# A four-stage sequence model in one kernel: pipeline streams shifted by a step, layer-norm means folded into the weights, and the state's weighing split in halves inside the recurrence's step

## The chip, the cores and the metric

The kernel runs on 1 core of a Trainium2 chip. The metric is device time in microseconds (us). Runs of one kernel agree here within 0.03%; the kernel before takes 3133.24 us (median of three, 3132.89 to 3133.72).

## The reference, cut to what matters

The input is 4 sequences of 1024 tokens with 128 features. Four blocks follow one another, each wrapped as x = layernorm(x + block(x)).

```python
# block 1: selective state space (256 inner channels, 16 states each)
h = exp(delta * A) * h + delta * b_t * u_t      # per channel and state, scanned over time
y = sum_over_states(h * c_t)                    # "the state's weighing"
# block 2: 16 routed experts (top 2) plus one shared expert, width 64 / 352
# block 3: an LSTM with 20 units over 1024 steps, then Gaussian attention
g = xg_t + h @ W_hh.T
c = sigmoid(f) * c + sigmoid(i) * tanh(gg);  h = sigmoid(o) * tanh(c)
# block 4: four MoE layers (4 experts of width 512, top 2)
logits = x @ rw + rb;  vals = top2(softmax(logits)) renormalised
xhat = (x - mean(x)) * rsqrt(mean((x - mean(x))**2) + 1e-5)
h = gelu((xhat * g + b) @ w1 + b1);  y = h @ w2 + b2;  x = sum_e comb_e * (x + y_e)
```

## The kernel before, in words

Time is cut into 8 chunks of 128 tokens (all 4 sequences at once, so a tile is 128 features x 512 columns, float32). The LSTM is the backbone: its 1024 steps cannot be made parallel, so everything else is placed between them. The function `period(i)` writes, for each engine, the instruction order of 128 steps of the LSTM (chunk i) and, between them, block 4 with the attention of chunk i-1 (`layer1`), block 2 of chunk i+1 (`layer0`), and the state-space scan of chunk i+2 (`scan`). Each stream is a Python generator that yields at the end of a slot; one slot holds one LSTM step. There is an opening (chunks 0 and 1 of blocks 1 and 2), periods 0 to 7, and a period 8 that has only `layer1`. Period 0 has no `layer1`, but it folds the layer-norm gain into w1 (`fold`). The scan runs in periods 0 to 5.

**A slot.** TensorE (PE) multiplies the last hidden state by w_hh (L905). ScalarE (ACT) takes the tanh of the gates (L915, L916). VectorE (DVE) does three small operations that end in the new cell (L929, L932, L935), ACT takes the cell's tanh (L919), and DVE writes the hidden state (L940), on which the next slot's PE waits. The tiles are p_turn (gates), cell, cell_t and hist.

**Block 4 in a period.** After 17 + q + 1 slots of attention come four layers of 23 slots. Five slots are the norm (mean by a matmul with mean_w, L623 and L625; centring on DVE, L372; square on ACT, L362; variance on PE; power -0.5 on GpSimd, L388; the product, L381). The routing decision lies beside it. Then come 18 slots of the experts: up matmul L656 into p_hid, Gelu L714, down matmul L666, and DVE's weighting L820 and sum L833.

**The scan in a period.** Sixteen slots of each layer (here called the heavy slots) carry 8 of the chunk's 32 scan steps. One scan step takes two slots, called a pair below. In the first slot DVE ends with the scan L1197 (state<-decay,drive). In the second it ends with the weighing L1206 (weighed<-state,rows). GpSimd (POOL) makes the next step's drive (L1135, then a small add L1139) and sums the weighed states into y (L1154). In the second slot of most pairs DVE also has one operation of block 4 (L820 or L833). The decays (ACT, L1226) are made in bursts in the norm's slots, and `layer0` advances in the slots that are not heavy.

Waits are semaphores. `put_drive` for step k+1 waits until scan k-1 is done, since two buffers take turns; `y` waits for the weighing.

Of the kernel before, what the change touches and what calls it, by code (L numbers as in the profile page):

```python
# [42 lines left out]
def body(nc, A, ctx, sem, out):  # L43
# [108 lines left out]
    w_router1 = sbuf("w_router1", [P, L * E1])  # L152
# [89 lines left out]
    fold_scaled = sem("r_fold_scaled")  # L242
    fold_stored = sem("r_fold_stored")
# [66 lines left out]
    g_step = sem("f1_step")  # L310
    g_comb = sem("f1_comb")
# [21 lines left out]
    def norm_pe(nm, n, src, ready, extra=None, early=None):  # L333
# [7 lines left out]
        if extra is not None:  # L341
            extra()
# [16 lines left out]
    def norm_act(nm, n):  # L359
        yield  # L360
        nc.scalar.wait_ge(nm.centred_done, n + 1)
# [6 lines left out]
    def norm_dve(nm, n, src, ready, dst):  # L368
        dve = nc.vector
        dve.wait_ge(*ready)  # L370
        dve.wait_ge(nm.mean_done, n + 1)
# [8 lines left out]
        dve.wait_ge(nm.centred_done, n + 1)  # L380
# [14 lines left out]
    def choose_dve(n, E, W, bank, bias, logit, left, top, mid, arg, half, mask, comb, tanh_, share_of, s_logit, s_step, s_arg, s_tanh, s_comb):  # L395
        dve = nc.vector
        dve.wait_ge(s_logit, n + 1)
        found = bank[:, 0:B * E].rearrange("p (b e) -> p b e", b=B)
# [15 lines left out]

# [6 lines left out]
        yield  # L421
# [14 lines left out]
    def layer0_pe(q):  # L436
# [24 lines left out]
        for u in range(U0):  # L461
# [32 lines left out]
    def layer0_act(q):  # L494
# [14 lines left out]
        yield  # L509
        for u in range(U0):  # L510
# [14 lines left out]
    def layer0_dve(q):  # L525
# [3 lines left out]
        yield from choose_dve(q, E0, E0, p_up, None, logit0, left0, top0, mid0, arg0, half0, mask0, comb0, tanh0, 0.25,  # L529
# [3 lines left out]
        nc.vector.tensor_scalar(share[:, :], share[:, :], 0.25, 0.25, ALU.mult, ALU.add).then_inc(share_ready, 1)  # L533
        yield
# [28 lines left out]
        weigh(U0 - 1)  # L563
        dve.wait_ge(down_done, (q + 1) * U0)
# [9 lines left out]
    LAYER = UN + 7  # L574
    att_slots = lambda q: 17 + q + 1
# [3 lines left out]
    def layer1_pe(q):  # L579
# [7 lines left out]
        for g in range(4):  # L587
            if g >= 2:
                pe.wait_ge(mup_taken, q * 4 + (g - 1))
            nc.tensor.matmul(p_hid[:, g % 2, :], w_mub[:, g, :], hist[:, q % 2, :, :], start=True, stop=True).then_inc(mup_done, 1)  # L590
            yield
# [4 lines left out]
        for i in range(q + 1):  # L596
# [3 lines left out]
            else:  # L600
                yield
# [12 lines left out]
        for _ in range(6):  # L614
            yield
# [3 lines left out]
        mm.then_inc(x3t_done, 1)  # L619
        yield  # L620
# [7 lines left out]
        for l in range(L):  # L628
# [42 lines left out]
    def layer1_act(q):  # L671
# [18 lines left out]
        for _ in range(9):  # L690
            yield
# [993 lines left out]
```

## Time and profile before

| | |
|---|---|
| median of three runs | 3133.24 us |
| profiled execution, its own time | 3143.73 us |
| its span | 3141.7 us |
| mean granted TensorE clock | 0.803 |
| busy: PE / DVE / ACT / POOL | 2537.0 / 1943.4 / 1386.7 / 1062.8 us |
| chain that ended last: PE / DVE / ACT / issue | 41% / 28% / 14% / 7% |

No engine is busy all the time: the LSTM's chain hands over between three of them in each slot. So what matters is read slot by slot: which engine's work ends last before the next hidden state. Starts of L905 mark the slots, and the stretches in the rows below begin and end at such starts. A "heavy" stretch is 16 slots and 8 scan steps long. A stretch between two heavy ones is 7 slots.

### The profile page before, as it was taken

What the parts mean: (1) busy time and instruction counts of PE and PEld (TensorE: products, weight loads), DVE (VectorE), ACT (ScalarE), POOL (GpSimd) and SP (SyncE); (2) the same over time, 40 slices, a digit from 0 to 9 for tenths busy, and PEclk for the clock granted to TensorE, in tenths of its full rate; (3) what the DMA queues carried; (4) which work ended last, traced back from release to release, by engine and by line L of the source; (5) the groups of instructions that cost most, each with busy time, mean ns of one, the idle gap of its engine ahead of it and who ended that gap; (6) DMA issues with size and microseconds to landing.
All of it is one profiled execution on the core that took longest, in us unless ns stands there. A gap on an engine that the chain in (4) does not pass through costs nothing.

```text
span 3141.7 us, 30770 instructions
## 1 busy us (share of the span) xinstructions
PE 2537.0 (81%) x7208; PEld 1271.2 (40%) x7208; DVE 1943.4 (62%) x6569; ACT 1386.7 (44%) x4620; POOL 1062.8 (34%) x913
## 2 busy tenths in 40 slices
PE   4776884479996989789886998788978997889598
PEld 1122443244444444344444443444444444444344
DVE  4857587357775777567766677577766555444422
ACT  3232433435544555445544554445534444444233
POOL 4735257104542445235432455244422001100200
PEclk7587655659996899878996899789978996788699
DMA  3231332003321233113220332122311220111021
GB/s 108 68 84 54 89 99 72 25 13 100 101 66 28 80 96 90 42 46 101 78 71 27 92 97 75 25 73 84 92 33 46 65 64 21 34 64 58 10 81 57
DMA packets 111774, 204.70 MB, mean 65 GB/s; under 512 B 14799, under 2 KB 24422, under 8 KB 111592
## 3 DMA queue, kind: packets, MB, share of 16 engines
q1 hardware_dynamic: 111592, 202.75, 22.1%
q8 instruction: 57, 0.93, 0.1%
q14 instruction: 125, 1.02, 0.1%
HBM read 195.36 MB, written 7.34 MB: 65 GB/s over the span
## 4 chain that ended last, share of the span: by engine, by line
PE 41%; DVE 28%; ACT 14%; issue 7%; POOL 1%; DVEq 0%; POOLq 0%; ACTq 0%
PE p_hid L656 8%; DVE state L1197 7%; PE p_turn L905 7%; PE p_misc L666 4%; ACT cell_t L919 4%; DVE cell L935 3%; DVE add_c L932 3%; PE p_acc L666 3%; DVE weighed L1206 2%; DVE p_turn L929 2%; PE p_misc L354 2%; PE p_gate L465 2%; DVE hist L940 2%; PE p_turn L475 1%; ACT cand L916 1%
## 5 line engine op out<-in xcount | busy, mean ns | idle before, releaser
L905 PEld LDWEIGHTS p_turn<-hist,w_hh 22*128 22x128 f32 x2048 | 371.6, 225 | 1148.2 <-DVE hist L940 1013.9
L905 PE MATMUL p_turn<-hist,w_hh 22*128 22x4 f32 x2048 | 457.3, 291 | 420.2 <-DVE hist L940 402.2
L656 PE MATMUL p_hid<-xhat,w 128*128 128x512 f32 x1024 | 581.8, 652 | 1.1 <-ACT hid L714 0.7
L919 ACT ACTIVATE cell_t<-cell 20x4 f32<-20x4 f32 x1024 | 207.7, 203 | 701.7 <-DVE cell L935 701.7
L1135 POOL TENSOR_TENSOR drive<-du,rows 128x512 f32<-128x512 f32 x256 | 473.4, 1849 | 63.2 <-DVE state L1197 44.9
L929 DVE SCALAR_TENSOR_TENSOR p_turn<-p_turn,cell 20x4 f32<-20x4 f32 x1024 | 170.7, 167 | 500.8 <-ACT p_turn L915 478.9
L714 ACT ACTIVATE hid<-p_hid,b1f 128x512 f32<-128x512 f32 x512 | 351.6, 687 | 243.1 <-PE p_misc L666 151.1
L388 POOL TENSOR_TENSOR n_rstd<-n_var,minus_half 128x4 f32<-128x4 f32 x56 | 62.0, 1108 | 1098.3 <-DVE n_var L376 1098.3
L1197 DVE TENSOR_TENSOR_SCAN state<-decay,drive 128x512 f32<-128x512 f32 x256 | 398.1, 1555 | 25.2 <-POOL drive L1139 15.7
L1154 POOL TENSOR_TENSOR y<-y,weighed 128x512 f32<-128x512 f32 x192 | 242.4, 1262 | 450.5 <-DVE weighed L1206 449.9
L940 DVE SCALAR_TENSOR_TENSOR hist<-p_turn,cell_t 20x4 f32<-20x4 f32 x1024 | 162.7, 159 | 275.6 <-ACT cell_t L919 275.6
L915 ACT ACTIVATE p_turn<-p_turn 96x4 f32<-96x4 f32 x1024 | 157.8, 154 | 349.1 <-PE p_turn L905 345.7
L666 PE MATMUL p_acc<-hid,w 128*128 128x512 f32 x512 | 275.3, 621 | 0.0
L666 PE MATMUL p_misc<-hid,w 128*128 128x512 f32 x512 | 264.1, 598 | 0.0
L1206 DVE TENSOR_TENSOR weighed<-state,rows 128x512 f32<-128x512 f32 x256 | 184.7, 722 | 7.9 <-DVE state L1197 0.5
L916 ACT ACTIVATE cand<-p_turn 32x4 f32<-32x4 f32 x1024 | 171.9, 168 | 25.2
L935 DVE SCALAR_TENSOR_TENSOR cell<-p_turn,add_c 20x4 f32<-20x4 f32 x1024 | 157.9, 154 | 35.3
L656 PEld LDWEIGHTS p_hid<-xhat,w 128*128 128x128 f32 x1024 | 160.3, 191 | 42.5 <-issue 26.5
L1169 PE MATMUL p_hid<-weighed,ident 128*128 128x512 f32 x128 | 113.7, 986 | 78.9 <-DVE weighed L1206 78.9
L1226 ACT ACTIVATE decay<-delta,a_neg 128x508 f32<-128x508 f32 x256 | 174.6, 710 | 2.2
L932 DVE SCALAR_TENSOR_TENSOR add_c<-p_turn,cand 20x4 f32<-20x4 f32 x1024 | 154.8, 151 | 31.6
L1139 POOL TENSOR_TENSOR drive<-drive,kc 128x4 f32<-128x4 f32 x256 | 143.2, 559 | 20.1
(204 smaller groups left out, 3161.5 us busy)
## 6 DMA issues: line engine op xcount, KB each, us to landing
rows<-rows_dram SPq DMA_DIRECT2D x128, 512.0 KB, 5.0
w<-w_dram SPq DMA_DIRECT2D x128, 256.0 KB, 2.7
w<-in_w2T SPq DMA_DIRECT2D x128, 256.0 KB, 2.7
comb_b<-comb_dram SPq DMA_DIRECT2D x64, 512.0 KB, 4.7
rows<-comb_dram SPq DMA_DIRECT2D x128, 128.0 KB, 2.9
w<-in_w1T SPq DMA_DIRECT2D x16, 256.0 KB, 2.8
w_dram<-w SPq DMA_DIRECT2D x16, 256.0 KB, 2.4
out_xT<-result SPq DMA_DIRECT2D x8, 256.0 KB, 2.5
```

What stands on the lines that cost most here:

```text
L656: nc.tensor.matmul(p_hid[:, v % 2, :], w1[:, v // FB, (v % FB) * P:(v % FB + 1) * P], xhat[:, :], start=True, stop=True).then_inc(g_h, 1)
L666: nc.tensor.matmul((p_misc1, p_acc1)[e % 2][:, :], w2[:, e, f, :], hid1[:, w % 2, :], start=(f == 0), stop=(f == FB - 1)).then_inc(g_y, 1)
L714: nc.scalar.activation(hid1[:, v % 2, :], p_hid[:, v % 2, :], ACT.Gelu, bias=b1f[:, l * UN + v:l * UN + v + 1]).then_inc(g_gelu, 1)
L905: nc.tensor.matmul(gate_bank(i)[:, :, t:t + 1], w_hh[:, :], before, start=False, stop=False, skip_group_check=True).then_inc(gates_done, 1)
L919: nc.scalar.activation(cell_t[64:64 + PE_, :], cell[32:32 + PE_, :], ACT.Tanh, scale=0.5).then_inc(cell_tanh, 1)
L929: nc.vector.scalar_tensor_tensor(out=gate(32), in0=gate(32), scalar=1.0, in1=cell[32:32 + PE_, :], op0=ALU.add, op1=ALU.mult).then_inc(kee ...
L932: nc.vector.scalar_tensor_tensor(out=add_c[32:32 + PE_, :], in0=gate(0), scalar=1.0, in1=cand[0:PE_, :], op0=ALU.add, op1=ALU.mult).then_i ...
L935: nc.vector.scalar_tensor_tensor(out=cell[32:32 + PE_, :], in0=gate(32), scalar=0.5, in1=add_c[32:32 + PE_, :], op0=ALU.mult, op1=ALU.add) ...
L1135: nc.gpsimd.tensor_tensor(flat(drive[:, n % 2, :, :]), du[:, j, :], rows[:, (u * S + s_) % ROWS, 0, :], ALU.mult).then_inc(driven, 1)
L1154: nc.gpsimd.tensor_tensor(y[:, j, :], y[:, j, :], weighed[:, n % 2, :], ALU.add).then_inc(y_summed, 1)
L1197: nc.vector.tensor_tensor_scan(flat(state[:, n % 2, :, :]), flat(decay[:, n % RING, :, :]), flat(drive[:, n % 2, :, :]), 0.0, ALU.mult, AL ...
L1206: nc.vector.tensor_tensor(weighed[:, n % 2, :], flat(state[:, n % 2, :, :]), rows[:, (u * S + s_) % ROWS, 1, :], ALU.mult).then_inc(weighe ...
```

## The change

- **Weighing.** The 512 columns of L1206 are split in two halves of 256. In periods they are written by a new stream, `mamba_gap_dve`, that stands between the LSTM's cell and its output: half one in the slot after the scan, half two one slot later, ahead of the next scan. Only half two signals `weighed_done`. In the opening the weighing stays whole.
- **The sum into y.** GpSimd (or PE in the opening) now sums step k-1 after it has made the drive of step k+1; before, it summed step k.
- **Centred weights.** The fold in period 0 subtracts the column mean from w1 (one matmul and one subtraction more for each of 16 tiles), so block 4's norm needs no centring: a fifth column in the router's matmul gives the mean, the square is taken of x itself, and the variance is E[x^2] + eps - mean^2. The two matmuls with mean_w and the centring go from the four layers; the last norm keeps them.
- **Order.** The transposes of the routing weights and their copy move behind the first up matmul; two DVE operations of the attention become one; decays stand ahead of the layer's work in their slots; `layer0` starts at slot 1 (was 4) and skips the last slot of each layer; several streams have a yield more or less.

```diff
     def choose_dve(...):
...
                                        in1=logit[:, :, 0:E], op0=ALU.mult, op1=ALU.add).then_inc(s_arg, 1)
-
+        yield
         nc.vector.memset(top[:, :, 2:8], -NEVER).then_inc(s_step, 1)
...
     def layer1_pe(q):
...
-            ln = norm_pe(n1, q * NL + l, src, (n1.src_ready, q * NL + l + 1), logits, (lambda: mean_of_two(n)) if l else None)
-            for s_ in range(5):
-                next(ln)
-                if s_ == 4:
-                    pe.wait_ge(g_comb, n + 1)
...
+            pe.wait_ge(n1.src_ready, q * NL + l + 1)
+            for j in range(B):
+                mm = nc.tensor.matmul(p_hid[:, 0, j * (E1 + 1):(j + 1) * (E1 + 1)], tile(src, j), w_router1[:, l, :],
+                                      start=True, stop=True)
+            mm.then_inc(g_logit, 1)
+            yield
+            pe.wait_ge(n1.square_done, q * NL + l + 1)
...
     def layer1_act(q):
...
+            nc.scalar.activation(n1.square[:, :], src, ACT.Square).then_inc(n1.square_done, 1)
...
     def layer1_dve(q):
...
+            nc.vector.scalar_tensor_tensor(out=n1.var[:, :], in0=p_acc1[:, 448:448 + B], scalar=EPS, in1=mean1[:, :],
+                                           op0=ALU.add, op1=ALU.subtract).then_inc(n1.var_taken, 1)
...
+            nc.vector.tensor_tensor(xhat[:, :], src, p_misc1[:, :], ALU.mult).then_inc(n1.out_done, 1)
...
     def lstm_dve(i):
...
             nc.vector.scalar_tensor_tensor(out=cell[32:32 + PE_, :], in0=gate(32), scalar=0.5,
                                            in1=add_c[32:32 + PE_, :], op0=ALU.mult, op1=ALU.add).then_inc(cell_done, 1)
+            yield
             dve.wait_ge(cell_tanh, n + 1)
...
     def mamba_scan_pool(u, early):
         pool = nc.gpsimd
+
+        def sum_y(k):
+            n, j = u * NS + k, k % NB
+            pool.wait_ge(weighed_done, n + 1)
+            if k < NB:
+                pool.wait_ge(y_begun, u * NB + j + 1)
+            else:
+                pool.wait_ge(y_summed, n - 1)
+            nc.gpsimd.tensor_tensor(y[:, j, :], y[:, j, :], weighed[:, n % 2, :], ALU.add).then_inc(y_summed, 1)
+
         for k in range(NS):
             n, j = u * NS + k, k % NB
             if k + 1 < NS:
                 put_drive(u, k + 1)
             yield
-            if not early:
...
+            if not early and k:
+                sum_y(k - 1)
+            yield
+        if not early:
+            sum_y(NS - 1)
...
+    def weigh_state(u, k, at, to):
...
+        cols = slice(at * CH, to * CH)
+        mm = nc.vector.tensor_tensor(weighed[:, n % 2, cols], flat(state[:, n % 2, :, :])[:, cols],
+                                     rows[:, (u * S + s_) % ROWS, 1, cols], ALU.mult)
+        if to == B:
+            mm.then_inc(weighed_done, 1)
+
+    def mamba_gap_dve(u):
+        for k in range(NS):
+            yield
+            weigh_state(u, k, 0, B // 2)
+            yield
+            weigh_state(u, k, B // 2, B)
...
     def fold_pe():
...
+            pe.wait_ge(fold_grown, k + 1)
+            if k:
+                pe.wait_ge(fold_scaled, k)
+            nc.tensor.matmul(p_misc1[:, :], mean_w[:, :], w1[:, k % E1, :], start=True, stop=True).then_inc(fold_mean, 1)
...
     def fold_dve():
...
+            dve.wait_ge(fold_mean, k + 1)
+            nc.vector.tensor_tensor(w1[:, k % E1, :], w1[:, k % E1, :], p_misc1[:, :], ALU.subtract).then_inc(fold_scaled, 1)
...
-    L0_AT = 4
+    L0_AT = 1
+    BURST = {LAYER - 1: 1, 0: 1, 1: 2, 2: 2, 3: 2}
...
             next(lstm, None)
+            o = (slot - att) % LAYER
+            heavy = layer1 is not None and slot >= att and NORM + 1 <= o < LAYER - 1 and slot < tail
+            if u < NCH:
+                if layer1 is None and soft[1] > SOFT and done["gap"] <= SCAN:
+                    advance(gap, "gap", SCAN)
+                elif layer1 and (heavy or slot == tail):
+                    advance(gap, "gap", SCAN)
+            next(lstm, None)
...
-            if layer0 and not (heavy and slot < CH) and slot >= (L0_AT if layer1 else 0):
+            last = layer1 is not None and att < slot < tail and o == LAYER - 1
+            if layer0 and not ((heavy or last) and slot < CH) and slot >= (L0_AT if layer1 else 0):
                 next(layer0, None)
```

**DVE in one pair of heavy slots.** Before: keep, add, cell, output (hist), then the layer's sum and the weighing; the second slot ends in the scan.

```order
L929 SCALAR_TENSOR_TENSOR p_turn<-p_turn,cell 20x4
L932 SCALAR_TENSOR_TENSOR add_c<-p_turn,cand 20x4
L935 SCALAR_TENSOR_TENSOR cell<-p_turn,add_c 20x4
L940 SCALAR_TENSOR_TENSOR hist<-p_turn,cell_t 20x4
L833 TENSOR_TENSOR part<-part,terms 128x512
L1206 TENSOR_TENSOR weighed<-state,rows 128x512
L929 SCALAR_TENSOR_TENSOR p_turn<-p_turn,cell 20x4
L932 SCALAR_TENSOR_TENSOR add_c<-p_turn,cand 20x4
L935 SCALAR_TENSOR_TENSOR cell<-p_turn,add_c 20x4
L940 SCALAR_TENSOR_TENSOR hist<-p_turn,cell_t 20x4
L1197 SCALAR_TENSOR_TENSOR state<-decay,drive 128x512
```

The same pair after the change (the line numbers are those of the changed kernel: L1282 is the weighing, L1264 the scan, L876 the sum).

```order
L978 SCALAR_TENSOR_TENSOR p_turn<-p_turn,cell 20x4
L981 SCALAR_TENSOR_TENSOR add_c<-p_turn,cand 20x4
L984 SCALAR_TENSOR_TENSOR cell<-p_turn,add_c 20x4
L1282 TENSOR_TENSOR weighed<-state,rows 128x256
L990 SCALAR_TENSOR_TENSOR hist<-p_turn,cell_t 20x4
L876 TENSOR_TENSOR part<-part,terms 128x512
L978 SCALAR_TENSOR_TENSOR p_turn<-p_turn,cell 20x4
L981 SCALAR_TENSOR_TENSOR add_c<-p_turn,cand 20x4
L984 SCALAR_TENSOR_TENSOR cell<-p_turn,add_c 20x4
L1282 TENSOR_TENSOR weighed<-state,rows 128x256
L990 SCALAR_TENSOR_TENSOR hist<-p_turn,cell_t 20x4
L1264 SCALAR_TENSOR_TENSOR state<-decay,drive 128x512
```

The weighing has left its place behind the sum; its two halves stand ahead of the output in both slots, and the second half is two instructions ahead of the next scan.

**POOL in the heavy slots**, after the change; the rows read as before it, with L1135, L1139 and L1154 for L1188, L1192 and L1204.

```order
L1188 TENSOR_TENSOR drive<-du,rows 128x512 [waits m_scan_done,m_rows_loaded0]
L1192 TENSOR_TENSOR drive<-drive,kc 128x4 [waits m_kc_done,m_driven]
L1204 TENSOR_TENSOR y<-y,weighed 128x512 [waits m_y_summed,m_weighed_done]
L1188 TENSOR_TENSOR drive<-du,rows 128x512 [waits m_scan_done,m_rows_loaded1]
L1192 TENSOR_TENSOR drive<-drive,kc 128x4 [waits m_kc_done,m_driven]
```

What moved is the step that the sum belongs to: behind the drive of step k+1 it is now step k-1's, whose weighing ends just ahead of scan k.

**PE at the start of a layer's norm**, before:

```order
L623 MATMUL p_misc<-part,mean_w 128x512
L625 MATMUL p_misc<-terms,mean_w 128x512
L634 MATMUL p_hid<-w_router,xl 128x4 x4
L475 MATMUL p_turn<-hid0w,w_down 128x512
L905 MATMUL p_turn<-hist,w_hh 128x4
```

and after:

```order
L645 MATMUL p_hid<-w_router,xl 128x5 x4
L470 MATMUL p_up<-mid_x,w_up 128x512
L952 MATMUL p_turn<-hist,w_hh 128x4
L651 MATMUL p_acc<-mean_w,esig 128x1 x4
L476 MATMUL p_turn<-hid0w,w_down 128x512
```

The two 512-column matmuls with mean_w are gone from the slot; `layer0`'s matmuls stand in it as before.

## Rows read from the trace of the kernel before

**Rows 1.** The page: granted TensorE clock by 40 slices of the span, in tenths.

```profile
PEclk7587655659996899878996899789978996788699
```

**Rows 2.** The scan's line: count, duration ns (min/median/max), first and last start.

```profile
L1197 DVE TENSOR_TENSOR_SCAN state<-decay,drive x256: 1210/1392/2289, 53.3 to 2300.0; 128x512 f32<-128x512 f32 x128
```

**Rows 3.** Windows of period 3: length, busy by engine (PE, PEld, DVE, ACT, POOL), clock.

```profile
1392.98:1431.38 38.40, 34.73 (x92) 14.75 (x93) 30.42 (x86) 19.73 (x72) 26.57 (x21) 1.00 0.36 112
1431.38:1457.32 25.94, 24.13 (x65) 12.39 (x65) 15.10 (x63) 13.25 (x36) 3.72 (x4) 0.68 0.14 44
1457.32:1495.62 38.30, 34.73 (x94) 14.75 (x93) 29.79 (x85) 19.37 (x72) 26.57 (x21) 1.00 0.44 122
1495.62:1515.97 20.35, 18.11 (x65) 9.18 (x65) 14.48 (x63) 12.78 (x36) 4.22 (x4) 0.92 0.11 41
1515.97:1554.71 38.74, 34.73 (x92) 14.75 (x92) 30.43 (x86) 20.21 (x74) 26.58 (x21) 1.00 0.39 122
...
1575.41:1612.29 36.88, 34.74 (x93) 14.76 (x93) 30.22 (x87) 18.33 (x72) 24.34 (x19) 1.00 0.33 97
```

**Rows 4.** Windows: period 0 with fold and layer0; its 11 last scans; period 6, heavy.

```profile
364.34:476.96 112.62, 97.26 (x239) 54.45 (x239) 91.73 (x220) 40.53 (x154) 54.36 (x47) 0.55 0.32 96
...
495.95:541.50 45.55, 12.87 (x45) 10.94 (x45) 35.65 (x111) 17.28 (x83) 42.32 (x33) 0.50 0.12 37
...
2413.15:2447.99 34.84, 34.03 (x92) 14.75 (x93) 14.42 (x71) 17.70 (x64) 0.00 (x0) 1.00 0.26 79
```

**Rows 5.** Timeline of one pair of heavy slots: start us, duration us, engine.

```profile
1534.51 0.16 DVE L940 SCALAR_TENSOR_TENSOR hist<-p_turn,cell_t 20x4 f32<-20x4 f32 x1 [0.27 <-ACT cell_t L919]
...
1534.70 0.69 DVE L833 TENSOR_TENSOR part<-xl,terms 128x512 f32<-128x512 f32 x1
...
1535.28 0.16 ACT L915 ACTIVATE p_turn<-p_turn 96x4 f32<-96x4 f32 x1
1535.31 0.69 DVE L1206 TENSOR_TENSOR weighed<-state,rows 128x512 f32<-128x512 f32 x1
...
1536.07 1.26 POOL L1154 TENSOR_TENSOR y<-y,weighed 128x512 f32<-128x512 f32 x1 [0.62 <-DVE weighed L1206]
...
1536.83 0.16 DVE L940 SCALAR_TENSOR_TENSOR hist<-p_turn,cell_t 20x4 f32<-20x4 f32 x1 [0.27 <-ACT cell_t L919]
1537.02 1.39 DVE L1197 TENSOR_TENSOR_SCAN state<-decay,drive 128x512 f32<-128x512 f32 x1
...
1537.29 2.18 POOL L1135 TENSOR_TENSOR drive<-du,rows 128x512 f32<-128x512 f32 x1
...
1538.44 0.17 DVE L929 SCALAR_TENSOR_TENSOR p_turn<-p_turn,cell 20x4 f32<-20x4 f32 x1
...
1538.83 0.15 DVE L935 SCALAR_TENSOR_TENSOR cell<-p_turn,add_c 20x4 f32<-20x4 f32 x1
...
1539.25 0.16 DVE L940 SCALAR_TENSOR_TENSOR hist<-p_turn,cell_t 20x4 f32<-20x4 f32 x1 [0.27 <-ACT cell_t L919]
```

**Rows 6.** Timeline: a scan that starts just behind a GpSimd operation.

```profile
1403.20 1.26 POOL L1135 TENSOR_TENSOR drive<-du,rows 128x512 f32<-128x512 f32 x1
1403.34 2.20 DVE L1197 TENSOR_TENSOR_SCAN state<-decay,drive 128x512 f32<-128x512 f32 x1
```

**Rows 7.** Timeline of the opening: a weighing behind a drive.

```profile
202.26 1.56 POOL L1135 TENSOR_TENSOR drive<-du,rows 128x512 f32<-128x512 f32 x1 [4.10 <-DVE state L1197]
202.61 1.75 DVE L1206 TENSOR_TENSOR weighed<-state,rows 128x512 f32<-128x512 f32 x1
```

**Rows 8.** Timeline where a layer's norm begins.

```profile
1436.12 1.97 PE L623 MATMUL p_misc<-part,mean_w 128*128 128x512 f32 x2
...
1437.92 1.02 PE L625 MATMUL p_misc<-terms,mean_w 128*128 128x512 f32 x2
...
1439.05 0.69 DVE L372 TENSOR_TENSOR mdrive<-xl,p_misc 128x512 f32<-128x512 f32 x1 [1.68 <-PE p_misc L625]
```

More of the change, by code:

```diff
@@ L517, in layer0_act @@
                 yield
+        for _ in range(3):
+            yield
+        yield from norm_act(n0, 2 * q + 1)
         yield
-        yield from norm_act(n0, 2 * q + 1)
         act.wait_ge(xt_done, q + 1)
@@ L586, in layer1_pe @@
         pe.wait_ge(xm_done, min(q + 3, NCH))
[L587 to L590, printed above, removed]
+        for k, g in enumerate((0, 2, 1, 3)):
+            if k >= 2:
+                pe.wait_ge(mup_taken, q * 4 + (k - 1))
+            nc.tensor.matmul(p_hid[:, k % 2, :], w_mub[:, g, :], hist[:, q % 2, :, :], start=True, stop=True).then_inc(mup_done, 1)
             yield
@@ L613, in layer1_pe @@
         mm.then_inc(ss_summed, 1)
-        for _ in range(6):
+        for _ in range(7):
             yield
@@ L657, in layer1_pe @@
                                      start=True, stop=True).then_inc(g_h, 1)
+                if v == 0:
+                    pe.wait_ge(g_comb, n + 1)
+                    for j in range(B):
+                        mm = nc.tensor.transpose(tile(p_acc1, j)[0:E1, :], comb1[:, j, :], ident[:, :])
+                    mm.then_inc(g_combT, 1)
                 if v >= 2:
@@ L689, in layer1_act @@
             yield
-        for _ in range(9):
+        for _ in range(10):
             yield
@@ L803, in layer1_dve @@
         mm.then_inc(nt_done, 1)
-        yield
-        yield
+        for _ in range(3):
+            yield
         for l in range(L):
@@ L892, in layer0_pool @@
         yield from norm_pool(n0, 2 * q)
-        for _ in range(6 + 3 * U0):
+        for _ in range(9 + 3 * U0):
             yield
@@ L990, in mamba_pre_pe @@
         yield
+        z(1, p_misc1)
         yield
@@ L1425, in period @@
         ends = att + L * LAYER + 5 if layer1 else 0
-        done = dict(scan=0, leave=0, fold=0, pre=0, soft=0)
+        done = dict(scan=0, leave=0, fold=0, pre=0, soft=0, gap=0)
         fold_slots = 3 * L * E1 + 12 + 1
@@ L1439, in period @@
             next(lstm, None)
+            o = (slot - att) % LAYER
[6 more added lines that the diff above has]
+            next(lstm, None)
+            if u < NCH and layer1 and att - 1 <= slot < tail - 2:
+                for _ in range(BURST.get(o, 0)):
+                    next(burst, None)
             if layer1:
                 next(layer1, None)
-            o = (slot - att) % LAYER
-            heavy = layer1 is not None and slot >= att and 6 <= o < LAYER - 1 and slot < tail
-            if layer0 and not (heavy and slot < CH) and slot >= (L0_AT if layer1 else 0):
+            last = layer1 is not None and att < slot < tail and o == LAYER - 1
+            if layer0 and not ((heavy or last) and slot < CH) and slot >= (L0_AT if layer1 else 0):
                 next(layer0, None)
@@ L1606, in start @@
                 dve.sem_inc(h_ready, 1)
-            of = dict(soft=mamba_soft_dve, scan=mamba_scan_dve, leave=mamba_leave_dve, fold=fold_dve, layer0=layer0_dve,
+            of = dict(soft=mamba_soft_dve, scan=mamba_scan_dve, gap=mamba_gap_dve, leave=mamba_leave_dve, fold=fold_dve, layer0=layer0_dve,
                       layer1=layer1_dve, lstm=lstm_dve)
```

247 lines of the change are left out of this document (142 added, 105 removed).

## The prediction, made before the changed kernel was run

> **What bounds the kernel now.** I read three views in this order. The slices of the page show the clock going up and down, so the run is a row of stages with different limits [rows 1]. Windows cut at the starts of L905 then give the length of each stage. The timeline of two slots, last, shows what ends last in one.
>
> A heavy stretch has 16 slots and 8 scan steps. The four of period 3 take 38.40, 38.30, 38.74 and 36.88 us, 152.3 us together [rows 3], or 4.76 us for a pair of slots. In period 6, which has no scan, the same 16 slots take 34.84 us with PE busy for 34.03 [rows 4]. So PE's floor is 4.36 us a pair, and the scan costs 0.40 us on top. Five periods have such stretches, 20 in all, with 160 pairs: of the 256 scans [rows 2], 64 lie in the opening and 32 in period 0.
>
> Within a pair DVE ends last in both slots [rows 5]. In the scan's slot the hidden state is out at 1536.99, the scan runs from 1537.02 to 1538.41, keep starts 0.03 us later, the cell ends 0.54 us after that, and the next hidden state is out at 1539.41: 2.42 us. In the other slot the sum (0.69) and the weighing (0.69) stand in a row ahead of keep, and the slot takes 2.32 us. ACT's gates end at 1535.44, before DVE is free.
>
> **The rows that decide: DVE and GpSimd hold each other up.** The scan of [rows 5] takes 1.39 us, with the last 0.31 us of GpSimd's y beside its start; with nothing on GpSimd it is 1.21 us at the least [rows 2]. The drive that GpSimd starts 0.27 us into it takes 2.18 us instead of 1.26 and ends 1.06 us after the scan: it has waited. In [rows 6] the order is reversed. The drive starts 0.14 us ahead of the scan and takes its plain 1.26, and the scan takes 2.20. In [rows 7] a weighing starts 0.35 us behind a drive and takes 1.75 us, ending 0.54 us after the drive. The LSTM's small operations, which read PSUM, run beside a drive at their usual 0.15 to 0.17 us [rows 5]. So an operation of DVE with two SBUF tensors that starts behind a GpSimd operation waits for its end.
>
> The Trainium skill (SBUF — State Buffer, "SBUF: two separate sides") states this as an exclusive lock that the first one holds for its whole instruction. By that rule too the next paragraph's order of starts is what matters; the trace agrees with it in both directions [rows 5 to 7].
>
> **The weighing in halves.** Half of L1206 is 256 columns. No row has that shape. Between the 0.16 us of a four-column operation and the 0.69 of 512 columns it is 0.42 us [rows 5]; the bounds are half of 0.69, 0.35, and all of it. The gap between cell and output is 0.27 us [rows 5], so an undisturbed half delays the output by 0.03 + 0.42 + 0.03 - 0.27 = 0.2 us.
>
> The Trainium skill (VectorE: DVE Perf Modes, "The TRN2 errata") gives 58 cycles plus one per column at 0.96 GHz for such an operation, 0.33 us for a half; its sum would be about 15 us lower. For 512 columns that is 0.59, and the rows show 0.69, so I keep to the rows.
>
> Now the order of starts in a pair after the change, counted from the output in the slot of scan k, time 0:
> - Half two of step k-1 ends 0.19 us before 0 (0.03 of hand-over and 0.16 for the output). It releases y(k-1) on GpSimd, which has long ended its drive. A weighing's end is followed by y's start in 0.07 us [rows 5], so y starts at -0.12 and the scan, at +0.03, is 0.15 us behind. That is the distance of [rows 6]. The scan takes 2.20 us, to 2.23.
> - The drive of step k+2 waits for this scan. It starts about 0.1 us later and runs its 1.26 us, to 3.59. Keep to cell take 0.03 + 0.54 us, so half one of step k asks at 2.83, behind the drive. It ends 0.27 us after the drive (0.54 of [rows 7] less half the columns), at 3.86. The output follows, to 4.05.
> - In the next slot the layer's operation (0.03 + 0.75 at most) covers the gates, which end 0.77 us after an output [rows 5]; keep starts at 0.81, the cell ends at 1.35, half two at 1.80, the output at 1.99. GpSimd is idle by then.
>
> The pair takes 4.05 + 1.99 = 6.04 us, of 8 in a stretch six with a layer operation and two 0.1 shorter: 48.1 against 38.1. What was removed, a 0.69 us weighing ahead of keep, is in this sum. Twenty stretches cost 20 x 10.1 = **+202 us**. Queued behind the held scan and half are the LSTM's own operations, so nothing hides it. The bounds are -52 us, if nothing collides (the first rival), and +240, if a half took 0.6.
>
> **Clock.** PE then works some 4.4 of 6.04 us, with an idle stretch of about 1.9 in each pair. The stretch 1431.38 to 1457.32 has PE busy 24.13 of 25.94 us at a granted 0.68, the heavy ones stand at 1.00 [rows 3]. At 1.2 GHz a pair of passes takes 1.97 us against 1.02 [rows 8], and a pair of slots would take about 8 us. If 15% of 20 x 48 us ran at that level it would cost 960 x 0.15 x (1 - 6.04/8) = **+35 us**. The bounds are 0 and 85 (35%).
>
> **Period 0.** No layer operation stands there, and the eleven last scans take 45.55 us, 4.14 us a pair [rows 4]. At 6.0 us they cost +20, four pairs ahead of them +5. In the first 112.62 us [rows 4] `layer0` operations stand between output and scan, so y has mostly run out by then. There the fold adds 16 subtractions of 0.69 us and 16 matmuls; PE, 86% busy at 0.55 of the clock, has little room. I take +8 (0 to 25). Sum **+33 us**.
>
> **The norm.** The mean's two matmuls take PE from 1436.12 to 1438.78, DVE sits idle 1.68 us for them, and the centring takes 0.69 [rows 8]. At full clock they are about 1.8 us, and they stand in the slot that begins a norm. The slot before it also loses `layer0`'s matmul, about 1.2 us. I count -3 us for each of 20 norms, -60; `layer0` comes back in the attention's first slots for +2 a period, +10. Period 6 and 7 give -14 (1.8 a norm, no more), period 8, where the norm is a bare chain, 4 x -1.8 = -8. Sum **-72 us** (bounds -110 and -40). What is late next is PE's logits and `layer0` matmul in the same slot. The mean's copy, its square and the fifth column are 0.2 us of DVE beside other work; the Square of x instead of the centred tile costs the same. The moved transposes lie behind an up matmul; the copy of the weights for the DMA is a slot later, and is first used five slots on: 0. The decays moved within their slots: 0, or +1 us a norm if they hold up the square.
>
> **The rest.** One 0.69 us operation of DVE fewer in each attention: 8 x -0.69 = **-5 us**. The later sum into y in the opening changes no wait, as step k-2 is still summed a step ahead of its buffer's next use: 0. The shifted yields of the pre and leave streams keep the number of slots: 0, give or take 5.
>
> **Sum.** 202 + 35 + 33 - 72 - 5 = +193 us on the profiled execution's 3143.73, 3337. That execution is 10.5 us above the median of 3133.24, so in the median's terms 3326.
>
> **Rivals.**
> 1. *No collision*: y or the scan gets in first without holding up the other, or the lock does not work at this distance. Then the scan's slot is 0.03 + 1.21 + 0.57 + 0.45 + 0.19 = 2.45 and the other 1.99, 4.44 a pair. PE's floor is 4.36, so a stretch is 35.5: -52 us. With +10 for period 0, no clock term and -77 for norm and attention: -119, **3014 us**. This is the other side. For it speaks that the weighing leaves DVE's longest slot; against it [rows 6], at nearly the same distance. It decides from 5.2 us a pair down: there 160 pairs cost 0.45 x 160 = 70 us, what the norm saves.
> 2. *Only the scan is held up* (the drive comes later than half one): 3.44 + 1.99 = 5.43 a pair, 43.4 a stretch, +106; with +15 of clock, +20 and -77: **3197 us**. [rows 7] speak against it, since half one asks 0.6 us after the scan and the drive needs only a semaphore.
> 3. *Only half one is held up*: 3.06 + 1.99 = 5.05, 40.2 a stretch, +42; with +5, +20 and -77: -10, **3123 us**. It needs GpSimd still busy when half two ends, and nothing in the order gives it work there.
>
> **Chances.** The forecast 0.78, rival 1 0.13, rival 2 0.05, rival 3 0.02, anything slower still 0.02. The forecast's own range is 3200 to 3430: the heavy stretches +180 to +220, the clock 0 to +85, the norm -110 to -40. Rival 2 lies at its edge, so the range starts at 3190; rivals 1 and 3 stay outside. About 0.2% can be told from no change here: faster 0.15, same 0.01, slower 0.84.
>
> **What would show it.** The scan's group in the periods at a mean near 2.2 us instead of 1.4; the weighing's halves in two kinds, 0.42 and about 1.0 us; y starting 0.1 to 0.2 us ahead of a scan; heavy stretches near 48 us with slots of 4.1 and 2.0 in turn; no L623 in layers 1 to 3, and stretches between heavy ones some 3 us shorter. Scans of 1.2 to 1.4 us and stretches of 36 us would make the prediction wrong by its first step; a clock of 1.00 in the heavy stretches would take away the clock's term alone.

## The result, and the profile after

The changed kernel takes 3416.7 us (median of four runs, 3414.01 to 3420.31) where the kernel before takes 3133.48 (3132.89 to 3136.19): a ratio of 1.0903, with a 95% interval of 1.0884 to 1.0922. It is slower by 283 us; 193 were forecast. The profiled execution is 3414.01 us, its span 3412.2, 270.5 above the span before. The first four runs of the kernel before agree within 0.11%; in the experiments below it takes 3127.14 to 3156.39 us, with medians of 3141.53 to 3146.63, so differences of a few tenths of a per cent between experiments mean little.

The page first: busy time by engine, the granted clock in 40 slices, and four groups (busy us, mean ns, idle time ahead and what ended most of it).

```profile
PE 2681.1 (79%) x7128; PEld 1336.5 (39%) x7128; DVE 2212.1 (65%) x6802; ACT 1398.1 (41%) x4620; POOL 906.0 (27%) x914
...
PEclk6686665578886888868886878968876898587788
...
L1264 DVE TENSOR_TENSOR_SCAN state<-decay,drive 128x512 f32<-128x512 f32 x256 | 522.5, 2041 | 23.8 <-POOL drive L1192 14.4
...
L1188 POOL TENSOR_TENSOR drive<-du,rows 128x512 f32<-128x512 f32 x256 | 348.3, 1360 | 311.5 <-DVE state L1264 294.6
...
L1204 POOL TENSOR_TENSOR y<-y,weighed 128x512 f32<-128x512 f32 x192 | 242.5, 1263 | 530.2 <-DVE weighed L1282 530.2
L1282 DVE TENSOR_TENSOR weighed<-state,rows 128x256 f32<-128x256 f32 (+1 forms) x448 | 325.4, 726 | 18.8 <-DVE state L1264 0.5
```

The scan's mean over all 256 is 2041 ns for 1555 before, its median 2200 for 1392 [rows 2]. Both means hold 64 scans of the opening at about 1.9 us; in the heavy stretches alone the mean is 2.17 us for 1.43, and 155 of the 160 scans there take over 2 us, for 14 before. GpSimd is busy for 157 us less than before: its drive no longer waits behind a running scan, it makes DVE wait. Its idle time ahead of y (530 us) is all put down to the weighing, that ahead of the drive (295 of 312) to the scan: each starts as soon as DVE signals. DVE's 269 us more of "busy" (2212.1 for 1943.4) are mostly time in which it is held up: 124 us in the scans and some 110 in the halves, whose split by itself costs about 0.15 us a step.

The timeline of a pair shows the order of starts.

```profile
1539.89 0.42 DVE L1282 TENSOR_TENSOR weighed<-state,rows 128x256 f32<-128x256 f32 x1
...
1540.35 0.16 DVE L990 SCALAR_TENSOR_TENSOR hist<-p_turn,cell_t 20x4 f32<-20x4 f32 x1
1540.39 1.26 POOL L1204 TENSOR_TENSOR y<-y,weighed 128x512 f32<-128x512 f32 x1 [2.00 <-DVE weighed L1282]
...
1540.66 2.08 DVE L1264 TENSOR_TENSOR_SCAN state<-decay,drive 128x512 f32<-128x512 f32 x1 [0.15 <-issue]
...
1542.88 1.26 POOL L1188 TENSOR_TENSOR drive<-du,rows 128x512 f32<-128x512 f32 x1 [1.23 <-DVE state L1264]
...
1543.34 1.08 DVE L1282 TENSOR_TENSOR weighed<-state,rows 128x256 f32<-128x256 f32 x1
1544.43 0.16 DVE L990 SCALAR_TENSOR_TENSOR hist<-p_turn,cell_t 20x4 f32<-20x4 f32 x1
...
1545.92 0.42 DVE L1282 TENSOR_TENSOR weighed<-state,rows 128x256 f32<-128x256 f32 x1
1546.37 0.16 DVE L990 SCALAR_TENSOR_TENSOR hist<-p_turn,cell_t 20x4 f32<-20x4 f32 x1
1546.42 1.26 POOL L1204 TENSOR_TENSOR y<-y,weighed 128x512 f32<-128x512 f32 x1 [1.94 <-DVE weighed L1282]
...
1546.56 2.20 DVE L1264 TENSOR_TENSOR_SCAN state<-decay,drive 128x512 f32<-128x512 f32 x1
```

Read it by starts. Half two ends at 1540.31; y starts 0.08 us later, the scan 0.27 us after y, and the scan ends 1.09 us after y. The drive starts 0.14 us after the scan's end; half one, 0.46 us behind the drive, takes 1.08 us and ends 0.28 after it. Half two, with an idle GpSimd, takes 0.42. The outputs end at 1540.51, 1544.59 and 1546.53: slots of 4.08 and 1.94 us. The scan at 1540.66 is one of two that start so late; the other 153 held scans start 0.14 to 0.2 us behind y, as the one at 1546.56 does, and take 2.20 us.

The windows of period 3 answer to [rows 3]: length, busy by engine, clock.

```profile
1502.52:1521.97 19.45, 18.48 (x55) 10.05 (x55) 11.22 (x56) 12.54 (x33) 2.45 (x3) 0.65 0.13 42
1521.97:1568.43 46.46, 36.03 (x94) 15.33 (x93) 40.90 (x93) 19.29 (x72) 19.51 (x21) 0.96 0.31 94
1568.43:1592.37 23.94, 22.43 (x59) 12.11 (x59) 13.37 (x62) 13.71 (x36) 2.46 (x3) 0.57 0.13 44
1592.37:1640.03 47.66, 36.03 (x94) 15.32 (x93) 42.51 (x94) 19.38 (x73) 20.77 (x22) 0.96 0.35 100
1640.03:1663.99 23.96, 22.37 (x58) 12.13 (x58) 13.37 (x62) 13.71 (x36) 2.46 (x3) 0.57 0.07 22
```

And two of period 0 answer to [rows 4]:

```profile
361.34:483.05 121.71, 96.28 (x252) 48.92 (x251) 110.56 (x247) 40.87 (x153) 46.12 (x50) 0.68 0.30 89
509.50:575.90 66.40, 12.84 (x45) 10.90 (x45) 53.36 (x121) 17.30 (x83) 27.57 (x29) 0.50 0.09 24
```

A heavy stretch went from about 38.1 to about 47.2 us, and its clock fell only to 0.96. The seven slots between two heavy stretches got longer together (71.87 us for 66.99 in period 3), although they hold less work: they stand at a clock of 0.57, which before was 0.68 to 0.92. The next table adds such windows up over each kernel's profiled execution (us; e1 to e7 are experiments, below).

| part | before | after | e1 | e2 | e5 | e6 | e7 |
|---|---|---|---|---|---|---|---|
| opening | 327.9 | 318.8 | 317.4 | 322.2 | 319.4 | 320.2 | 323.5 |
| period 0 | 318.4 | 361.8 | 331.1 | 352.0 | 328.8 | 330.5 | 329.3 |
| periods 1-5, heavy | 761.9 | 946.9 | 748.3 | 958.6 | 748.3 | 745.0 | 747.8 |
| periods 1-5, between (norm and last slots) | 443.1 | 459.4 | 444.3 | 432.7 | 420.4 | 435.6 | 416.3 |
| periods 1-5, attention and tail | 484.5 | 508.6 | 502.8 | 485.3 | 497.9 | 498.3 | 497.0 |
| period 6 | 303.5 | 315.4 | 319.6 | 307.7 | 309.5 | 305.5 | 311.0 |
| period 7 | 293.7 | 291.8 | 294.8 | 297.1 | 285.0 | 292.0 | 282.8 |
| period 8 | 208.7 | 209.4 | 209.5 | 209.5 | 210.3 | 209.5 | 210.4 |

### The profile page after: what moved, and what is told of

It reads as the page before. It is cut to its first block, busy times and chain, and to the rows that moved or that the text cites. A ratio compares the mean times of both kernels' runs of the same rounds, so it can differ in the third digit from the quotient of the medians.

```text
span 3412.2 us, 30859 instructions
## 1 busy us (share of the span) xinstructions
PE 2681.1 (79%) x7128; PEld 1336.5 (39%) x7128; DVE 2212.1 (65%) x6802; ACT 1398.1 (41%) x4620; POOL 906.0 (27%) x914
## 4 chain that ended last, share of the span: by engine, by line
PE 42%; DVE 33%; issue 8%; ACT 8%; POOL 1%; DVEq 0%; POOLq 0%; ACTq 0%
DVE state L1264 11%; PE p_hid L668 8%; PE p_turn L952 7%; DVE weighed L1282 5%; PE p_misc L685 3%; DVE add_c L981 3%; PE p_acc L685 3%; PE p_up L470 3%; PE p_gate L466 2%; DVE cell L984 2%; PE p_turn L476 2%; DVE hist L990 2%; PE p_misc L657 2%; ACT cell_t L968 2%; DVE p_turn L978 2%
## 5 line engine op out<-in xcount | busy, mean ns | idle before, releaser
L952 PEld LDWEIGHTS p_turn<-hist,w_hh 22*128 22x128 f32 x2048 | 388.9, 235 | 1309.8 <-DVE hist L990 1030.4
L952 PE MATMUL p_turn<-hist,w_hh 22*128 22x4 f32 x2048 | 475.2, 300 | 503.6 <-DVE hist L990 503.3
L668 PE MATMUL p_hid<-xhat,w 128*128 128x512 f32 x1024 | 602.3, 672 | 4.9 <-DVE xhat L857 4.9
L1264 DVE TENSOR_TENSOR_SCAN state<-decay,drive 128x512 f32<-128x512 f32 x256 | 522.5, 2041 | 23.8 <-POOL drive L1192 14.4
L1188 POOL TENSOR_TENSOR drive<-du,rows 128x512 f32<-128x512 f32 x256 | 348.3, 1360 | 311.5 <-DVE state L1264 294.6
L1204 POOL TENSOR_TENSOR y<-y,weighed 128x512 f32<-128x512 f32 x192 | 242.5, 1263 | 530.2 <-DVE weighed L1282 530.2
L1282 DVE TENSOR_TENSOR weighed<-state,rows 128x256 f32<-128x256 f32 (+1 forms) x448 | 325.4, 726 | 18.8 <-DVE state L1264 0.5
L685 PE MATMUL p_acc<-hid,w 128*128 128x512 f32 x512 | 283.8, 639 | 0.0
L932 POOL TENSOR_TENSOR n_rstd<-n_var,minus_half 128x4 f32<-128x4 f32 x32 | 32.4, 1011 | 800.8 <-DVE n_var L850 800.8
L466 PE MATMUL p_gate<-mid_x,w_gate 128*128 128x512 f32 x176 | 147.4, 933 | 15.5 <-DVE hid L564 13.2
```

What stands on the lines that cost most here:

```text
L668: nc.tensor.matmul(p_hid[:, v % 2, :], w1[:, v // FB, (v % FB) * P:(v % FB + 1) * P], xhat[:, :], start=True, stop=True).then_inc(g_h, 1)
L685: nc.tensor.matmul((p_misc1, p_acc1)[e % 2][:, :], w2[:, e, f, :], hid1[:, w % 2, :], start=(f == 0), stop=(f == FB - 1)).then_inc(g_y, 1)
L952: nc.tensor.matmul(gate_bank(i)[:, :, t:t + 1], w_hh[:, :], before, start=False, stop=False, skip_group_check=True).then_inc(gates_done, 1)
L1188: nc.gpsimd.tensor_tensor(flat(drive[:, n % 2, :, :]), du[:, j, :], rows[:, (u * S + s_) % ROWS, 0, :], ALU.mult).then_inc(driven, 1)
L1204: nc.gpsimd.tensor_tensor(y[:, j, :], y[:, j, :], weighed[:, n % 2, :], ALU.add).then_inc(y_summed, 1)
L1264: nc.vector.tensor_tensor_scan(flat(state[:, n % 2, :, :]), flat(decay[:, n % RING, :, :]), flat(drive[:, n % 2, :, :]), 0.0, ALU.mult, AL ...
```

## The experiments

Theory A, as the expectations call it, is the prediction's: GpSimd's y starts just ahead of the scan and holds it, and the drive then holds half one. Theory B is that the halves are harmless and the new norm and order cost the time. Each experiment gives the ratio to the kernel before in the same batch, with its 95% interval.

**e1: the weighing whole and in its old place**, the rest of the change kept.

```diff
-            if not early and k:
-                sum_y(k - 1)
+            if not early:
+                sum_y(k)
...
-            if early:
-                weigh_state(u, k, 0, B)
+            weigh_state(u, k, 0, B)
...
-            weigh_state(u, k, 0, B // 2)
...
-            weigh_state(u, k, B // 2, B)
```

> The changed kernel with the weighing whole and at its old place (behind the layer's operation) and GpSimd summing step k again, all else of the change kept. Theory A (DVE and GpSimd hold each other up: y ahead of the scan, the drive ahead of half one): scans fall from 2.20 back to about 1.4 us, the heavy stretches from 189 us a period to 152, period 0 loses some 35 us, so 3417 - 185 - 35 = about 3197 us. If the slow norms of the changed kernel come from the idle PE of its heavy stretches, they get faster too and it is 3150. Theory B (the halves are harmless, the new norm and order cost the time): within 20 us of 3417.

Measured: 3169.61 us against 3146.63, ratio 1.0069 (1.0044 to 1.0094). The heavy stretches fall from 946.9 to 748.3 us. So the weighing's new place explains nearly the whole loss; but what is left of the change, which the prediction priced at a gain of some 70 us, loses 0.7%. The time lies between the two that were expected, 3150 and 3197 us.

**e2: the weighing's part alone**, on the kernel before.

```diff
+            if not early and k:
+                sum_y(k - 1)
...
+    def mamba_gap_dve(u):
+        for k in range(NS):
+            yield
+            weigh_state(u, k, 0, B // 2)
+            yield
+            weigh_state(u, k, B // 2, B)
```

> The kernel before with only the halves between cell and output and GpSimd's sum one step later; norm, fold and order of before. Theory A: 160 pairs in periods 1 to 5 from 4.76 to 5.9 us, +185, and period 0 +30: about 3350 us, with scans at 2.20 us. Theory B: about 3135 to 3170 us (the halves' overflow of 0.2 us a slot at most). A third reading, in which half of the loss is the norm's, would also give 3350 here, but then e1_whole stays near 3197.

Measured: 3356.25 us, ratio 1.0668 (1.0637 to 1.0699), heavy stretches 191.7 us a period, mean of all scans 2057 ns. Most of the loss comes with this part alone. The whole change loses 9.0%, more than 6.7% and e1's 0.7% together. In the profiled executions the excess is 21 us (270 for 223 and 26), and the norm and last slots account for it: +16 us, for -10 in e2 and +1 in e1.

**e3: y held back until the scan is done**, so that nothing runs on GpSimd when the scan starts.

```diff
         def sum_y(k):
             n, j = u * NS + k, k % NB
+            if k + 1 < NS:
+                pool.wait_ge(scan_done, n + 2)
             pool.wait_ge(weighed_done, n + 1)
```

> The changed kernel, but GpSimd's sum of step k-1 also waits until scan k is done, so it cannot start ahead of that scan. Theory A, with two separate collisions: scans fall to 1.2 us, half one stays held up at about 1.1 us (now by y), a pair goes from 5.9 to about 5.05 us, 160 x -0.85 = -136, period 0 -12: about 3270 us. Theory B: no change, or a few us more for the later sum.

Measured: 3262.11 us, ratio 1.0363 (1.0334 to 1.0393). Its timeline:

```profile
1478.96 1.23 DVE L1266 TENSOR_TENSOR_SCAN state<-decay,drive 128x512 f32<-128x512 f32 x1
...
1480.32 1.26 POOL L1206 TENSOR_TENSOR y<-y,weighed 128x512 f32<-128x512 f32 x1 [2.16 <-DVE state L1266]
1480.80 1.06 DVE L1284 TENSOR_TENSOR weighed<-state,rows 128x256 f32<-128x256 f32 x1
```

The scan runs free in 1.23 us. Half one is now behind y, and ends 0.28 us after it. One collision of the two is gone, and with it 5.4% of the time (1.0903 to 1.0363). Not all of this is the collision's own: of the 153 us between the two profiled executions, 107 lie in the heavy stretches and 13 in period 0, but 31 in the norm and last slots, where the granted clock is 0.70 for 0.61.

**e8 and e9: the weighing whole, between cell and output of the next scan's slot.** Nothing then stands in the gap of the slot that the drive fills. In e9 y is free to start; e8 has e3's wait as well.

```diff
     def mamba_gap_dve(u):
...
             yield
-            weigh_state(u, k, 0, B // 2)
             yield
-            weigh_state(u, k, B // 2, B)
+            weigh_state(u, k, 0, B)
```

> The changed kernel with the weighing whole between cell and output, in the slot of the next scan alone (nothing in the other slot), and GpSimd's sum of step k-1 held until scan k is done. Collision theory: the scan runs free (1.2 us), GpSimd then does y and the drive in a row (2.6 us), and the weighing, asking some 3.5 us after the scan's start, meets only the tail of the drive: a pair of 4.6 to 4.9 us, heavy stretches of 147 to 156 us a period, total as e1_whole or a few us from it (3150 to 3185 us). If placing the weighing in the gap were itself what costs, it would stay near e3's 3262 us.

> The changed kernel with the weighing whole between cell and output in the slot of the next scan, none in the other slot, and GpSimd's sum free to start (no added wait). Collision theory: only the scan is held up (y starts 0.14 us ahead of it, scans at 2.20 us); the drive's end no longer meets a weighing. From the measured slots: the scan's slot 3.2 to 3.3 us, the other 2.3 (0.27 us of gap, 0.69 of weighing), a pair of 5.5 us, heavy stretches of 176 us a period, 13 us a period less than the changed kernel's 189: about 3345 us, ratio 1.065 to 1.072. If the two collisions did not add up one by one, it would stay at 1.09 or fall to 1.03.

Measured: e8 3168.85 us, ratio 1.0095 (1.0062 to 1.0127); e9 3312.7, ratio 1.0548 (1.0512 to 1.0584). The timeline of e9:

```profile
1492.39 0.69 DVE L1282 TENSOR_TENSOR weighed<-state,rows 128x512 f32<-128x512 f32 x1
1493.11 0.16 DVE L990 SCALAR_TENSOR_TENSOR hist<-p_turn,cell_t 20x4 f32<-20x4 f32 x1
1493.16 1.26 POOL L1204 TENSOR_TENSOR y<-y,weighed 128x512 f32<-128x512 f32 x1 [1.31 <-DVE weighed L1282]
1493.30 2.20 DVE L1264 TENSOR_TENSOR_SCAN state<-decay,drive 128x512 f32<-128x512 f32 x1
```

The weighing is free, y starts 0.14 us ahead of the scan, the scan is held. The heavy stretches came as expected (175 us a period for 176), the total 32 us below the expected 3345: period 0 is 16 us shorter than in the changed kernel, norm and last slots 9, attention and tails 7, and the expectation had counted none of these. With e3, e8 and the changed kernel this makes a square (the scan's time is the mean in the heavy stretches):

| heavy stretches, us a period | y waits for the scan | y free |
|---|---|---|
| whole weighing in the gap | e8: 151.5, scan 1.23 us | e9: 175, scan 2.17 us |
| halves in the gap | e3: 168, scan 1.23 us | after: 189, scan 2.17 us |

The held scan alone costs 23 us a period, the held half alone 16, both 38. Work in the gap by itself costs next to nothing: e8, whose weighing is still held, for about 0.4 us in 43 of the 160 pairs, stands beside e1's 149.7. So neither the split nor the gap costs much by itself; what costs is which engine starts first.

**e4 and e5: the two matmuls with mean_w put back, their result unread**, in layers 1 to 3; e4 on the changed kernel, e5 on e1.

```diff
+            if l:
+                pe.wait_ge(g_summed, n * E1 - 1)
+                nc.tensor.matmul(p_misc1[:, :], mean_w[:, :], part[:, :], start=True, stop=False, skip_group_check=True)
+                pe.wait_ge(g_weighted, n * E1)
+                nc.tensor.matmul(p_misc1[:, :], mean_w[:, :], terms[:, (E1 - 1) % 2, :], start=False, stop=True,
+                                 skip_group_check=True)
```

> The changed kernel with the two matmuls with mean_w put back at the start of the norm of layers 1 to 3, as work that nothing reads (the result stays the same). Clock theory (the emptier PE around the start of the norm lets the granted clock fall, and the whole norm then runs at the lower level): the stretches between heavy ones get a clock of 0.7 to 0.9 instead of 0.57 and stay at 24 us or fall to 22, so 3400 to 3420 us. Work theory (each matmul costs what it takes, no more): 24 norms x 1.8 to 3.7 us = 3460 to 3500 us.

> e1_whole (weighing whole, at its old place, all else of the change) with the two unread matmuls with mean_w at the start of the norm of layers 1 to 3. Clock theory: as e4 did against the changed kernel, the unread work gives time back: the stretches between heavy ones at a clock near 0.75 instead of 0.6, ratio to the kernel before 0.995 to 1.002 (e1_whole: 1.007). Work theory: 24 x 1.8 us or more on top, ratio 1.02.

Measured: e4 3398.6 us, ratio 1.0774 (1.0723 to 1.0824), below the changed kernel's 1.0903; e5 3129.74 us against 3141.53, ratio 0.9966 (0.9945 to 0.9988), below e1's 1.0069. By these ratios, adding work that nobody reads made both kernels 1% faster. In us it is 40 for e5 against e1 (1.3%), but only 18 for e4 against the changed kernel (0.5%), because the kernel before was 13 us slower beside e4; that pair is the weaker evidence. Windows of e1, the seven slots between heavy stretches, three times in period 3:

```profile
1440.88:1462.40 21.52, 18.54 (x58) 10.09 (x58) 13.70 (x63) 13.65 (x36) 4.38 (x6) 0.76 0.13 41
1499.80:1523.08 23.28, 21.02 (x59) 11.74 (x59) 13.97 (x63) 13.91 (x36) 4.38 (x6) 0.63 0.07 23
1560.47:1582.00 21.53, 18.48 (x58) 10.10 (x58) 13.61 (x63) 13.65 (x36) 4.38 (x6) 0.76 0.09 25
```

The same three in e5:

```profile
1427.08:1449.85 22.77, 21.64 (x62) 11.18 (x62) 14.07 (x63) 13.91 (x36) 4.38 (x6) 0.70 0.15 44
1487.27:1507.15 19.88, 17.15 (x62) 9.09 (x63) 13.97 (x63) 13.81 (x36) 4.38 (x6) 0.91 0.08 27
1544.56:1563.55 18.99, 17.08 (x62) 8.62 (x63) 13.61 (x63) 13.65 (x36) 4.39 (x6) 0.91 0.10 29
```

Summed, e1 takes 66.33 us with 175 matmuls and 58.03 us of busy PE, e5 61.64 us with 186 matmuls and 55.87 us busy. More matmuls in less busy time: the clock was granted at 0.91 in two of three stretches, in e1 in none. DVE's and ACT's busy times differ by under 0.5 us.

**e6 and e7: `layer0` allowed in the last slot of a layer again**; e6 on e1, e7 on e5.

```diff
-            if layer0 and not ((heavy or last) and slot < CH) and slot >= (L0_AT if layer1 else 0):
+            if layer0 and not (heavy and slot < CH) and slot >= (L0_AT if layer1 else 0):
```

> e1_whole with the block-2 stream (layer0) allowed again in the last slot of each layer, so that one 512-column matmul stands in the slot just ahead of the norm, as in the kernel before. Clock theory: the clock at the start of the norm stays up more often, the first two slots of the norm (5.2 and 4.2 us) shrink by 1 to 2 us in most of 24 norms, ratio 0.995 to 1.003. If only the work counts: the slot grows by about 1 us and an attention or tail slot shrinks by as much, ratio 1.005 to 1.009.

> e5 and e6 together: weighing whole, the unread mean matmuls, and layer0 in the last slot. If both work by the clock and add up: ratio 0.985 to 0.995. If one of them already fills the gap: as the better of the two. Work theory: the slowest of the three, 1.02.

Measured: e6 3135.06 us, ratio 0.9974 (0.9954 to 0.9994); e7 3108.11 us, ratio 0.9899 (0.987 to 0.9928). The unread matmuls give time back, `layer0`'s old place gives time back, and both together most. But e6 adds no work for PE, it only moves it (7128 matmuls, as e1 has), and its gain is not all the clock's: in the norm and last slots it is 9 us shorter than e1 at the same clock of 0.69, in period 6 it is 14 us shorter at 0.85 for 0.79. e7 beats the kernel before by 1.0% and is the best of all. Its three stretches of period 3:

```profile
1431.65:1452.16 20.51, 19.36 (x65) 10.19 (x65) 14.53 (x64) 13.72 (x36) 4.38 (x6) 0.83 0.19 52
1489.57:1509.65 20.08, 18.00 (x64) 9.72 (x64) 14.56 (x64) 14.21 (x37) 4.51 (x6) 0.92 0.09 27
1546.15:1567.60 21.45, 18.08 (x60) 9.91 (x61) 13.88 (x63) 13.22 (x35) 4.38 (x6) 0.77 0.08 26
```

## Why the prediction was right about the heavy stretches, and short by 90 us

**Heavy stretches: forecast +202, and +35 for the clock; measured +185.** The order of starts came as written: y, then the scan at 2.20, then the drive, then half one. The forecast slots were 4.05 and 1.99 us, the two in the timeline 4.08 and 1.94. Over all 160 pairs the mean is 5.92. The scan's slot takes 4.09 us in most pairs; but the last scan of a stretch has no drive behind it, its half one runs free in 0.42, and its slot takes 3.43. The other slot, behind the first of a stretch, takes 1.84 to 2.20, by what block 4 has in it. When half one asks later (0.72 us instead of 1.08, at 1549.73) the slot is as long, since the half still ends 0.28 us after the drive. A half took 0.42 us when free, as interpolated from the rows. The 0.33 comes from a general row of the cited section; the same section of the Trainium skill (VectorE: DVE Perf Modes, "The TRN2 errata") says that this row comes out too low and gives (columns + 151) cycles at 0.96 GHz for an fp32 tensor_tensor add, which for 256 columns makes 0.42. Rival 1 fell with the 155 scans of over 2 us. Rivals 2 and 3 exist as experiments: only the scan held, 5.46 us a pair in e9 (forecast 5.43, there with the halves split); only the half held, 5.25 in e3 (forecast 5.05, with half one behind a drive that starts on time; in e3 it stands behind y).

**Period 0: forecast +33, measured +43.** The eleven last scans take 66.40 us for 45.55 [rows 4], 6.04 a pair, for a forecast of 6.0. The stretch of [rows 4] with the fold took +9.1, against +8 forecast. The eight slots between the two windows took +7.5 (26.45 us for 18.99), against +5, and the 36 us ahead of both took +6, for which I had counted nothing. e1 puts the change without the weighing at +12.7 in this period.

**The norm: forecast -72, of it -60 for periods 1 to 5; measured +16 in their norm and last slots. This is the step that failed.** I took PE's matmuls off at what they cost and left the clock of what remained as it was. e1 puts +1 of the 16 to the change without the weighing, where -60 was forecast; beside it the weighing's new place adds the other 15. Part of what took the gain is the clock. The table has the three stretches of period 3, and in its last two columns all norm and last slots of periods 1 to 5, with the mean granted clock in them:

| kernel | matmuls | length, us | PE busy, us | clock | all norm and last slots, us | clock there |
|---|---|---|---|---|---|---|
| before | 194 | 66.99 | 61.80 | 0.68, 0.92, 0.84 | 443.1 | 0.81 |
| after | 176 | 71.87 | 67.13 | 0.57, 0.57, 0.57 | 459.4 | 0.61 |
| e2 | 193 | 63.99 | 58.68 | 0.78, 0.92, 0.83 | 432.7 | 0.83 |
| e3 | 175 | 67.36 | 61.83 | 0.62, 0.76, 0.57 | 428.2 | 0.70 |
| e4 | 188 | 68.50 | 63.33 | 0.60, 0.77, 0.83 | 450.4 | 0.70 |
| e1 | 175 | 66.33 | 58.03 | 0.76, 0.63, 0.76 | 444.3 | 0.69 |
| e6 | 177 | 66.09 | 59.09 | 0.76, 0.70, 0.70 | 435.6 | 0.69 |
| e5 | 186 | 61.64 | 55.87 | 0.70, 0.91, 0.91 | 420.4 | 0.80 |
| e7 | 189 | 62.04 | 55.44 | 0.83, 0.92, 0.77 | 416.3 | 0.79 |

In period 3, 19 matmuls fewer from before to e1 bought 0.7 us of 67. Over all norm and last slots the change without the weighing gave nothing at a clock of 0.69 for 0.81; with the unread matmuls back (e5) the clock is 0.80, and these slots are 24 us shorter than e1's and 23 shorter than before's, 1.1 for each of the 20 norms. So at least 24 of the 61 us between forecast and e1 go to the clock. For the other 37 the runs show no cause. `layer0`'s matmul, which I had counted at 1.2 us of the 3 for each norm, is a term that the runs refute: in its old place again it costs nothing there (e6 stands 9 us below e1, e7 4 below e5). What pays in e5 would then be what else left the slot, DVE's wait for the mean and the centring behind it; that is inferred, no run has it alone.

The clock is not the whole of it. At about 0.70 these slots take 428 us in e3, 436 in e6, 444 in e1 and 450 in e4, and this was not separated. Nor is it the emptier PE of the heavy stretches by itself that lowers the clock behind them: e2 has them as empty, keeps the norm of before, and stands at 0.83. The norm's change alone brings it to 0.69 (e1), and only on top of that does the weighing's new place lower it further, to 0.61: this is where the two parts are worse together.

I had priced the clock in the heavy stretches, at +35, and there it stayed at 0.96; it fell between them, where I had not looked for it.

That the granted clock answers to PE's work is shown by e4 and e5, and by e7 against e6: each adds the same unread matmuls, stands at a clock 0.09 to 0.11 higher in these slots, and is shorter. Which pattern of work it takes is not shown. In e7 the last stretch stands at 0.77 with fewer matmuls than the two ahead of it; in e5 the first at 0.70 with as many as the two behind.

**The rest.** Attention and tails of periods 1 to 5 took +24 (forecast -5, and +10 for `layer0` in the attention's first slots); e1 has +18, so most of it does not come from the weighing. Period 6, without any scan, took +12 for a forecast of -7; there too e5 gives 10 us back against e1, at a clock of 0.84 for 0.79, so the clock has a share. Period 7 took -2 for the same -7. Period 8 was forecast at -8 and took +0.7. The causes in these four parts stay open. The opening was 9 us shorter where 0 was forecast.

**The sum.** Taken from the profiled executions: 185 + 43 + 42 for all other parts = +270. Forecast were 202, 33 and -42 (norm, rest and clock), so the errors are -17, +10 and +84. Put where it was forecast, in the heavy stretches, the clock's +35 makes their error -52, and that of all other parts +119. The two offset each other: the norm lies outside its own bounds of -110 to -40, and the total is inside the range partly by luck, because the room left for a clock that did not fall in the heavy stretches took up a norm that brought no gain. The remaining 13 of the 90 us are the profiled executions: before's stood 10 us above its median, after's 3 us below.

## What to carry to other kernels

- Ask of each DVE operation with two SBUF tensors what GpSimd starts just ahead of it. A signal to GpSimd given by the instruction just ahead of a long DVE operation lets GpSimd in first, and the DVE operation then pays most of GpSimd's duration: here 0.97 us (2.20 for 1.23) behind an operation of 1.26. Have GpSimd wait for the long operation (e3, e8); giving the signal behind it should do the same, which no run tried.
- A matmul taken out of a stretch in which the clock varies is not worth its duration until the granted clock of what remains has been read in a run. Where the clock falls, work for PE can be cheaper in than out (e5, e7).
- When a change has two parts, run each alone: here one lost 6.7%, and hid that the other, with the mean's matmuls left in and `layer0` in its old place, gains 1%.

## What the runs showed of the hardware that was not expected

Unread matmuls made a kernel faster: 1.0069 to 0.9966 (e1 to e5) and 1.0903 to 1.0774 (after to e4), with the granted clock between the heavy stretches of period 3 going, in the second pair, from 0.57 in all three to 0.60, 0.77 and 0.83. PE was busy for 94% of the stretch at 0.57 (22.43 of 23.94 us), so a high busy share does not go with a high clock: at the lower level, 1.2 GHz, the same matmul is busy for twice as long [rows 8].

The Trainium skill (SBUF — State Buffer, "SBUF: two separate sides") calls the sharing of DVE and GpSimd an exclusive lock held for the whole instruction. The runs agree in every order. A scan behind y takes 2.20 us for 1.23 and ends 1.08 to 1.09 us after it; a half behind drive or y takes 1.06 to 1.08 for 0.42 and ends 0.28 after it; a drive behind a scan takes 2.18 for 1.26 and ends 1.06 after it [rows 5]. Behind GpSimd the distance goes with the DVE operation (1.08 us for the scan, 0.28 for a half, 0.54 for the whole weighing of [rows 7]), whichever GpSimd operation was first.
